# Table products and squares read straight from PSUM, the feed-forward once per batch, and a new order on every engine

## The reference, cut to what matters

```python
x = shift_tokens(x)                     # half of the channels one token down
q, k, v = split(x @ Wqkv[l], 3)         # 16 heads of 64
q = l2norm(q) * qs ; k = l2norm(k) * ks # norm over the 64 of a head
q = q * cos * scale + rotate_half(q) * sin * scale ; k = ... * inv
sim = q @ k.T * 8                       # windows of 32 tokens, keys: own and previous window
x = x_in + softmax(mask(sim)) @ v @ Wo[l]
xn = layernorm(shift_tokens(x))
a, gate = split(xn @ W1[l] + b1[l], 2)  # 2 x 341
x = x + (a * gelu(gate)) @ W2[l] + b2[l]
```

## Time and profile before

| | |
|---|---|
| median of 3 runs | 2977.41 us (2975.38 to 2978.07) |
| profiled execution | 2978.97 us, span 2977.2 us, mean granted TensorE clock 0.977 |
| busy, share of the span | PE 89%, weight loads 59%, DVE 69%, ACT 65%, POOL 55% |
| squares of the six layers (one per slot) | 96, first at 843.8 us, last at 2900.1 us |
| table loads on ACT in the six layers | two per slot, 1283 ns each |
| DMA | 112.65 MB in all, mean 38 GB/s |

### The profile page before, as it was taken

How to read it: one execution, slowest core, us unless ns; L and a number is a source line. 1 busy time by engine, 2 the same in 40 slices (tenths; PEclk the granted TensorE clock), 3 DMA queues, 4 the chain that set the end, 5 groups by cost and what they waited for, 6 DMA issues and landing times.

```text
span 2977.2 us, 64423 instructions
## 1 busy us (share of the span) xinstructions
PE 2639.6 (89%) x23097; PEld 1760.7 (59%) x23097; DVE 2064.9 (69%) x3311; ACT 1929.3 (65%) x3411; POOL 1649.6 (55%) x1188
## 2 busy tenths in 40 slices
PE   5787788999979999999999999999999999999995
PEld 2343345777746666666666666666666666666664
DVE  6898995555556767677676777767677676767764
ACT  3233232333357778787777878777787877778784
POOL 1342441000047777676777767677776777767672
PEclk9998999999989999999999999999999999999997
DMA  2000001000011121212112121211212121121211
GB/s 100 1 0 0 1 0 47 0 0 0 0 34 47 41 54 46 56 39 56 46 39 56 46 56 39 56 46 39 56 46 56 39 54 48 39 56 46 54 41 33
DMA packets 86713, 112.65 MB, mean 38 GB/s; under 512 B 60944, under 2 KB 62096, under 8 KB 85904
## 3 DMA queue, kind: packets, MB, share of 16 engines
q1 hardware_dynamic: 86672, 112.20, 14.3%
HBM read 29.28 MB, written 1.05 MB: 10 GB/s over the span
## 4 chain that ended last, share of the span: by engine, by line
ACT 26%; DVE 13%; POOL 12%; PE 9%; issue 5%; DMA 5%; SPq 1%; POOLq 0%; DVEq 0%; ACTq 0%
POOL f_qkr L1041 10%; ACT f_sq L1162 6%; DVE f_den L1229 5%; DMA f_xsC<-f_x 4%; ACT L1165 4%; ACT L1166 3%; ACT f_qT L1132 3%; ACT f_kT L1132 3%; DVE f_ssq L1268 3%; ACT f_Pr L1118 3%; PE f_psA L1399 2%; POOL f_Pr L1029 2%; PE f_psA L1393 2%; PE f_psO L1383 2%; ACT f_oT L1114 2%
## 5 line engine op out<-in xcount | busy, mean ns | idle before, releaser
L1035 POOL TENSOR_TENSOR f_m<-f_m 128x1024 f32<-128x1024 f32 x192 | 637.8, 3342 | 241.9 <-DVE f_m L1250 241.9
L1250 DVE TENSOR_TENSOR f_m<-f_qkraw,f_tab 128x2048 f32<-128x2048 f32 x192 | 433.5, 2299 | 480.7 <-POOL f_tab L1054 470.7
L1399 PE MATMUL f_psA<-f_W,f_xT 128*128 (+1 forms) x1152 | 605.8, 622 | 12.9 <-issue 8.1
L1029 POOL TENSOR_TENSOR f_Pr<-f_Pr,f_rden 128x384 f32<-128x384 f32 x384 | 310.1, 828 | 372.3 <-DVE f_rden L1231 372.3
L1041 POOL TENSOR_TENSOR f_qkr<-f_m,f_rn 128x1024 f32<-128x1024 f32 x192 | 361.0, 1901 | 0.9 <-DVE f_rn L1281 0.9
L208 POOL TENSOR_TENSOR m_HC<-m_Hs,m_Ct 128x512 f32<-128x512 f32 x128 | 163.8, 1279 | 299.6 <-DVE m_Hs L349 299.6
L1362 PE MATMUL f_psP<-ident,f_Pr 128*96 128x128 f32 x1536 | 238.1, 278 | 100.6 <-POOL f_Pr L1029 65.8
L1362 PEld LDWEIGHTS f_psP<-ident,f_Pr 128*96 128x96 f32 x1536 | 156.4, 127 | 267.8 <-POOL f_Pr L1029 149.6
L1125 ACT ACTIVATE f_qkraw<-f_psA 128x512 f32<-128x512 f32 x384 | 228.7, 596 | 110.0 <-PE f_psA L1399 110.0
L1101 ACT ACTIVATE f_PT<-f_psP 96x512 f32<-96x512 f32 x384 | 228.5, 595 | 84.4 <-PE f_psP L1362 79.3
L1383 PEld LDWEIGHTS f_psO<-f_PT,f_V 96*64 96x64 f32 x6144 | 217.7, 138 | 100.9 <-issue 89.3
(11 more groups left out here) (172 smaller groups left out, 5160.1 us busy)
## 6 DMA issues: line engine op xcount, KB each, us to landing
f_V<-f_Vt SPq DMA_DIRECT2D x96, 384.0 KB, 4.3
f_V<-f_Vt SPq DMA_DIRECT2D x96, 256.0 KB, 3.6
f_W<-in_f_W SPq DMA_DIRECT2D x48, 381.5 KB, 3.8
f_V<-f_Vt SPq DMA_DIRECT2D x48, 128.0 KB, 4.6
f_xsA<-xall SPq DMA_DIRECT2D x97, 32.0 KB
f_xsA<-xall SPq DMA_DIRECT2D x97, 31.8 KB
f_xsC<-f_x SPq DMA_DIRECT2D x96, 32.0 KB
f_xsC<-f_x SPq DMA_DIRECT2D x96, 31.8 KB
```

The source lines that it names most:

```text
L1029: pool.tensor_tensor(pv, pv, rv.unsqueeze(3).broadcast_to([P, 2, 2, KEYS]), ALU.mult).then_inc(Pr_ready[g][j], 1)
L1035: pool.tensor_tensor(mv[:, 0], mv[:, 0], mv[:, 1, :, ::-1, :], ALU.add).then_inc(rot_done[j], 1)
L1250: dve.tensor_tensor(m12[:, j, :, :].rearrange("p m (h d) -> p m h d", d=DH), rv.unsqueeze(1).broadcast_to([P, 2, H, DH]), tab[:, t, j, :, ...
L1399: pe.matmul(psA[n % 2][:, :], xT[:, t, :], weights(i, W_QKV + n * 512, 512), start=True, stop=True).then_inc(A_full[n_fill], 1)
```

## The change: what it does

1. **Squares and products from PSUM.** The copy `f_qkraw` and the 2048-wide square are gone. ACT squares each projection straight out of its PSUM bank (four of 512 columns). DVE then multiplies the same bank by the tables: four instructions of 2 x 512 results, each behind the square of its bank, and only then is the bank free for the next fill. The sum of squares follows at once.
2. **POOL.** The rotation writes `f_qkr`, now double-buffered by tile, in two instructions of 512 results in place of one of 1024; the scaling is in place. The table for the next tile is written behind the rotation. The gate (L1062) is gone. The sum with b2 goes into `xall` itself.
3. **Feed-forward per batch.** It runs on 256 tokens, transposed: hidden units on partitions. Even slots (t = 0) do stage D: two transposes of `f_hatC`, one ACT pass to `f_xnT`, three gate products (`w1(1, c)`), three Gelus with the bias as an operand. Odd slots do stage E: three products for a (`w1(0, c)`), three `scalar_tensor_tensor` on DVE ((a + bias) x gelu, straight out of PSUM to `f_hT`), six products with W2, one addition to `xall`. The three transposes of the hidden units and their copies are gone. W1 and its biases have a buffer of their own, loaded once per batch by SP behind E's last reader (128 x 688), and the shares of the other weights shrink from 763 to 593 columns.
4. **Orders.** Scores of the first head group come ahead of the last transposed fill of q/k; projection 4 and the transposed tokens come behind the scores of the second group; on ACT the Gelu stands behind the first head group's exponentials, in even slots only, and the logarithm and exponential of the norms behind it; `evacuate_v(1)` stands near the slot's end. `times_v` alternates between the two halves of the output partitions with each matmul.

Core of the diff (waits and helpers that only follow from it are left out):

```diff
-                dve.wait_ge(ga_full[n], du + 1)
-                dve.tensor_tensor(ga[:, n, :], psD[n][:, 0:FF], weights(di, W_B1 + n * FF, FF), ALU.add)
+                def gated(c):
+                    src, j = bank_of(c)
+                    if c != 1:
+                        dve.wait_ge(a_full[j], i - 1)
+                    dve.scalar_tensor_tensor(out=hT[0:FC[c], c, :], in0=src[0:FC[c], :], scalar=bias_col(c)[0:FC[c], :],
+                                             in1=ge[0:FC[c], c, :], op0=ALU.add, op1=ALU.mult)
+                def table_products(n):
+                    j = n // 2
+                    if n % 2 == 0:
+                        at_least(dve, rot_done[j], u)
+                    dve.wait_ge(squared[n], u + 1)
+                    half = slice((n % 2) * 512, (n % 2) * 512 + 512)
+                    dve.tensor_tensor(m12[:, j, :, half].rearrange("p m (h d) -> p m h d", d=DH),
+                                      psA[n % 2][:, :].rearrange("p (h d) -> p h d", d=DH).unsqueeze(1).broadcast_to([P, 2, H // 2, DH]),
+                                      tab[:, t, j, :, :].unsqueeze(2).broadcast_to([P, 2, H // 2, DH]), ALU.mult).then_inc(A_free[n], 1)
...
-                    act.activation(qkraw[:, n * 512:(n + 1) * 512], psA[n % 2][:, :], ACT.Copy).then_inc(A_free[n], 1)
+                    act.activation(sq[:, n * 512:(n + 1) * 512], psA[n % 2][:, :], ACT.Square).then_inc(squared[n], 1)
...
+                    exponentials(0)
                 if "D" in stages:
-                    act.activation(ge[:, :], ga[:, 1, :], ACT.Gelu).then_inc(ge_ready, 1)
+                    for c in range(3):
+                        act.activation(ge[0:FC[c], c, :], src[0:FC[c], :], ACT.Gelu, bias=bias_col(3 + c)[0:FC[c], :]).then_inc(ge_ready, 1)
                     act.preload_act_table_set(LN_EXP)
...
-                pool.tensor_tensor(mv[:, 0], mv[:, 0], mv[:, 1, :, ::-1, :], ALU.add).then_inc(rot_done[j], 1)
+                pool.tensor_tensor(qv[:, :, 0, :], mv[:, 0, :, 0, :], mv[:, 1, :, 1, :], ALU.add)
+                pool.tensor_tensor(qv[:, :, 1, :], mv[:, 0, :, 1, :], mv[:, 1, :, 0, :], ALU.add).then_inc(rot_done[j], 1)
...
+                if "E" in stages and not (isinstance(i, int) and i > ITERS):
+                    sp.wait_ge(h01_ready, (i - 1) * 2)
+                    sp.wait_ge(h2_ready, i - 1)
+                    load_up_projection(i - 1)
...
+                    if "D" in stages:
+                        pe.wait_ge(ge_ready, (i - 1) * 3)
+                    if "E" in stages:
+                        pe.wait_ge(h2_ready, i - 1)
+                    transpose_tokens(u + 1, i + t, 1 - t)
+                    project(4)
```

More of the change, by code:

```diff
@@ L798, in window_layers @@
     GH = H // 2
+    FC = [min(P, FF - c * P) for c in range(3)]
+    T2 = TPB * P
     with ExitStack() as ctx:
@@ L825, in window_layers @@
         rn = sb("f_rn", [P, 2 * H])
-        qkr = sb("f_qkr", [P, 2 * INNER])
+        qkr = sb("f_qkr", [P, 2, 2 * INNER])
         Vt = sb("f_Vt", [P, 2, INNER])
@@ L870, in window_layers @@
         kprev_ready = sem("f_kprev_ready")
-        m12_done = [sem(f"f_m12_done{j}") for j in range(2)]
-        sq_ready = sem("f_sq_ready")
+        squared = [sem(f"f_squared{n}") for n in range(4)]
         ssq_ready = sem("f_ssq_ready")
@@ L1189, in slot @@
                     act.activation(rn0[:, :], lnq[:, :], ACT.Exp, bias=consts[:, 1:2], scale=-0.5).then_inc(rn0_ready, 1)
+                    evacuate_tokens(u + 1, 1 - t)
+                    evacuate_v(0)
+                if "B" in stages:
+                    evacuate_probs(0, 0)
+                    exponentials(1)
+                    evacuate_probs(0, 1)
                 if "C" in stages:
@@ L1194, in slot @@
                     act.activation(rstdC[:, :], lnC[:, :], ACT.Exp, scale=-0.5).then_inc(rstdC_ready, 1)
+                if "A" in stages:
+                    evacuate_v(1)
                 if "B" in stages:
@@ L1253, in slot @@
-                if "D" in stages:
-                    weights_here(dve, di, share_of(W_2))
-                    add_bias(1)
-                    add_bias(0)
+                    for n in range(4):
+                        table_products(n)
+                    dve.wait_ge(squared[3], u + 1)
+                    dve.tensor_reduce(ssq[:, :], sq[:, :].rearrange("p (h d) -> p h d", d=DH), axis=AX.X, op=ALU.add).then_inc(ssq_ready, 1)
+                if "E" in stages:
+                    dve.wait_ge(ge_ready, (i - 1) * 3)
+                    gated(2)
@@ L1269, in slot @@
+                if "E" in stages:
+                    gated(0)
+                    gated(1)
                 if "C" in stages:
@@ L1378, in times_v @@
                         pe.wait_ge(V96_ready[q], (i + (1 if q == 0 else 0)) * n_dma)
-                    for n in range(4):
-                        h = 4 * j + n
-                        hh_ = 8 * g + h
-                        for half in range(2):
+                    for pair in range(2):
+                        for half, n in ((0, 2 * pair), (0, 2 * pair + 1), (1, 2 * pair), (1, 2 * pair + 1)):
+                            h = 4 * j + n
+                            hh_ = 8 * g + h
                             ins = pe.matmul(psO[(h % 2) * DH:(h % 2) * DH + DH, h // 2, half * HQ:(half + 1) * HQ],
@@ L1399, in project, with w1 @@
                     pe.matmul(psA[n % 2][:, :], xT[:, t, :], weights(i, W_QKV + n * 512, 512), start=True, stop=True).then_inc(A_full[n_fill], 1)
+                def w1(n, c, full):
+                    ins = pe.matmul(bank_of(c)[0][0:FC[c], :], W1[:, n * FF + c * P:n * FF + c * P + FC[c]], xnT[:, :], start=True, stop=True)
+                    if c > 0:
+                        ins.then_inc(full[bank_of(c)[1]], 1)
                 if "A" in stages:
@@ L1481, in slot @@
                     p = psD[0]
-                    for c in range(3):
-                        n = min(P, FF - c * P)
-                        ins = pe.matmul(p[:, 0:D], hT[0:n, c, :], weights(di, W_2 + c * D, D)[0:n, :], start=(c == 0), stop=(c == 2))
+                    for tt in range(TPB):
+                        for c in range(3):
+                            ins = pe.matmul(p[:, T2 + tt * D:T2 + (tt + 1) * D], hT[0:FC[c], c, tt * P:(tt + 1) * P],
+                                            weights(i - 2, W_2 + c * D, D)[0:FC[c], :], start=(c == 0), stop=(c == 2))
                     ins.then_inc(w2_full, 1)
@@ L1541, in host_layout @@
     w["f_W"] = pack.reshape(P, DEPTH, B, SHARE)
+    up_proj = np.zeros((P, DEPTH, W1_COLS), f)
+    for l in range(DEPTH):
+        up_proj[:, l, 0:2 * FF] = x["L0_ffn_W1"][l]
+        for n in range(2):
+            for c in range(3):
+                m = min(P, FF - c * P)
+                up_proj[0:m, l, 2 * FF + 3 * n + c] = x["L0_ffn_b1"][l][n * FF + c * P:n * FF + c * P + m]
+    w["f_W1"] = up_proj
     half = np.arange(0, DH, 2, dtype=f)
```

314 lines of the change are left out of this document (152 added, 162 removed).

## The result

| | before | after |
|---|---|---|
| median | 2976.39 us (2974.80 to 2978.07, 4 runs) | 2959.40 us (2958.28 to 2969.38, 4 runs) |
| ratio, 95% interval | | 0.995 (0.9928 to 0.9973) |
| profiled execution | 2978.97 us, span 2977.2 | 2969.38 us, span 2967.6 |
| even slot, mean of 46 in the profiled execution | 21.67 us | 22.24 us: 21 at 21.76, 25 at 22.49 to 22.72 |
| odd slot, mean of 45 in the profiled execution | 21.80 us | 20.96 us |

What follows compares the result with a forecast made beforehand. A closed DVE-POOL ring was taken to bound the 21.7 us slot, PE nearly full behind it. Even 21.9 plus odd 20.7 makes 42.6 against 43.4 us: -0.85 x 46 = -39, so 2937 us (range 2885 to 3000).

Steps and rivals of the forecast that it cites:

- the sum for the even slot: Slots with stage D: exponentials at 13.15 us plus 8.7 us behind them make 21.9 us.
- the ~1.3 us ahead of the token transposes: Sign in even slots: PE waits about 1.3 us there on f_ge, held for the last Gelu.
- ACT's chain: Even slot from first exponentials: ACT's loads, Gelus, norms, tokens, V and probabilities run as one chain, 8.7 us including times_v.
- The odd slot: Slots with stage E: PE's steps sum to 20.6 us, PE hardly ever late, so 20.7 us.
- Head and tail: Outside the loop: one feed-forward fewer ahead, a serial stage E more behind; taken as 0 (-3 to +4 us).
- The ring: DVE and POOL waiting on each other: 15.6 + 6.1 = 21.7 us sets the old slot; the early table removes it.
- Rival 1, late tile: f_hatC in odd slots waits behind POOL's scaling, PE's transposes late: +1.4 us a pair, 3005 us; chance 0.15.
- Rival 2, POOL held: DVE's new products hold POOL as the old ones do: pair 44.5 to 45.4, 3030 to 3070 us; chance 0.05.
- Rival 3, column halves at once: Alternating output halves in times_v run truly at once and halve it: pair 40.3, 2835 us; chance 0.05.
- Rival 4, no gain: W1 2 us late, or square-and-product bank ring 0.2 us a fill slower, uses up 0.85 us: 2975 us; chance 0.10.

Runs made afterwards that it cites:

- f1: Changed kernel plus eight unread 384-column matmuls on PE ahead of its wait for the Gelus in even slots; 2942.3 us, 0.9881 of the kernel before.
- f3: Changed kernel with ACT's fourth copy of transposed q/k and first exponentials moved behind the Gelus and their table loads; 2905.3 us, 0.9758 of the kernel before.
- g1: Changed kernel with Identity in place of Gelu and no table loads (gelu left out); 2855.9 us, 0.9585 of the kernel before.
- h2: Changed kernel with projection 4 ahead of PE's wait for the Gelus in even slots, no work added; 2955.2 us, 0.9919 of the kernel before.
- b1: Kernel before the change, with only POOL's next table moved behind the rotation; 2976.7 us, 0.9997 of the kernel before.
- b3: Kernel before the change, with Identity for Gelu and no table loads; 2957.9 us, 0.9931 of the kernel before.
- b4: Kernel before the change, with the table behind the rotation, Identity for Gelu and no table loads; 2928.6 us, 0.9833 of the kernel before.
- b2: Kernel before, table behind the rotation, rotation written from f_m to double-buffered f_qkr, DVE's products not waiting for the scaling; 3190.0 us, 1.0711 of the kernel before.
- g2: Changed kernel with times_v back in the order of heads, both key halves of a head together; 2967.3 us, 0.9967 of the kernel before.
- h1: f3 with projection 4 ahead of the second group's scores and projection 5 where 4 stood, in even slots; 2904.9 us, 0.9752 of the kernel before.

## Why the prediction was off, step by step

- **The failed step: the sum for the even slot was made at full clock.** PE "idles almost 3 us", it said, and the ~1.3 us ahead of the token transposes were priced as nothing but waiting. They were 1.68 us, and in 25 of 46 turns the granted clock falls to half around their end. That term is missing from the sum: 46 x 0.48 = 22 us in the profiled execution, 17 to 20 by the medians, shown by f1 (full clock, 2942 us). No rival named it. With it the forecast would have been 2954 to 2959; the rest of the miss is in the points below. The time did lie in the range of 2885 to 3000, but its upper part was kept for a late tile, which did not come.
- **The even slot at full clock**: 21.87 against 21.9, counted as the prediction counts. First exponentials 13.4 us after the start of projection 0 (13.15 predicted), token transposes 16.8 (16.6). ACT's chain sets it: f3, g1 and h2's quiet slots show it. PE's waits in it were 1.68 us for the last Gelu, 0.59 ahead of `f_psP` and 0.34 for `f_xnT`.
- **The odd slot**: 20.85 against 20.7, counted in the same way. PE has no wait over 0.3 us in it, as predicted; the steps' times were off. From start to start a set of transposed probabilities takes 0.53 (0.44 taken: +0.34 for four), the six projections 5.94 (+0.18), the four fills of transposed q/k 2.03 (+0.15), the four `times_v` 0.1 more; Wo, W2 and the three products for a take 0.5 less together. Wo is 1.79 us from start to start: the 1.95 in the sum was its duration in the row. 0.15 x 45 = 7 us, and with the even slot the pair is 42.72 against 42.6; against that the pair of the kernel before was 43.47 us, not 43.4.
- **Head and tail**: ahead of the fifth slot -13.7, behind the last +16.0: +2.3, within the -3 to +4. Of the tail 56 us are at half clock, 41 before.
- **The ring**: read rightly as closed, wrongly as the only bound. ACT's chain ran beside it at nearly the same length (b1: nothing; b1, b3, b4 together). The profile of the kernel before already hinted at it: in the chain that ended last ACT has 26% of the span, DVE 13% and POOL 12%, and the two table loads 4% and 3%. And "The next table is now made behind the rotation, not behind the scaling, so DVE need not wait for POOL's tail" named the wrong edit: with it alone DVE waits 4.32 us for the scaling (b1). What frees DVE is that the rotation leaves `f_m`; with products from SBUF that made the kernel 7% slower (b2). That products from PSUM alone turn this round was not run by itself.
- **Rival 1, late tile**: did not occur. `f_hatC` took 0.64 us behind the addition, at 1731.31, and PE's transposes came 0.96 us into the even slot; no wait of PE in the loop (over 0.1 us) ended on `f_hatC`.
- **Rival 2, POOL held**: did not occur; scaling 1.9, rotations 1.27, as the earlier trace rows had suggested. b2 shows what the old products do to the scaling. The Trainium skill ("GPSIMD Engine Reference", section 1, Specifications) names contention with VectorE instructions that have two SBUF inputs; b2's 7.80 and 5.81 us agree. It does not name products with one input in PSUM; here these took 2.36 us beside the scaling and 2.35 beside a rotation.
- **Rival 3, column halves at once**: 16 matmuls take 0.69, before 0.73; g2 puts it at 8 us, not 142.
- **Rival 4, no gain**: W1 and the bank ring were not late (none of PE's waits over 0.2 us in the loop is put down to them); more than half of the expected gain was lost, but to the clock.
- Left open: the profiled execution took 2969 us, the other three 2958 to 2960. How many dips they had is not recorded; their mean granted clocks were 0.963 to 0.966, against 0.960 in the profiled one, so it had more time at half clock than they. What decides in which turn a dip comes was not found either.

In terms of the forecast, with slots cut at the sums of squares: odd slots -38 (forecast -45), quiet even slots +4 (+9), dips +22 (0), head and tail +2 (0) in the profiled pair.

The best version here is f3 (2905 us; h1 the same): the changed kernel with its Gelus ahead of the fourth copy. With them there the change is worth 74 us; where they stood took 54 to 57 of these back, 37 by the length of ACT's chain (f1 to f3) and 17 to 20 by the clock (the changed kernel to f1).
